# Graph layers on one core: the 0/1 matrices of destination lanes made in the attention loops, f32 sums without a split

## What is computed

```python
x = layernorm(x + segment_sum(exp(-weight)[:, None] * x[dst], src))         # messages, by source
q, k, v = x @ Wq.T + bq, x @ Wk.T + bk, x @ Wv.T + bv                        # 4 heads of 16
s = (sum(q[dst] * k[src]) / 4 + edge_attr @ We.T + be) * exp(log_temp)       # one score an edge and head
x = layernorm(x + layernorm(x + softmax_by_dst(s) * v[src] summed by dst, times Wo))
e = leaky_relu((x @ W_l)[src] + (x @ W_r)[dst], 0.2) @ att                   # second attention, one head
x = layernorm(x + softmax_by_dst(e) * (x @ W_l)[src] summed by dst + bias)
x = layernorm(x + two layers of mean over the neighbours)
```

## Time and profile before

| | |
|---|---|
| time, median of 3 runs | 5168.92 us (5147.55 to 5176.96) |
| profiled execution, first to last instruction | 3717.5 us |
| what the median has beyond that span | 1451.4 us |
| busy: TensorE, weight loads, VectorE, ScalarE, GpSimd | 58%, 44%, 70%, 21%, 53% |
| granted clock of TensorE, mean | 0.69 |
| message stage | about 205 to 715 us |
| sums by source | 715 to 1020 us |
| first attention stage | 1098 to 2204 us |
| second attention stage | 2327 to 3473 us |

### The profile page before, as it was taken

The page is one execution under the profiler, slowest core; times in us unless marked ns, Lnnn a source line. Parts: engine busy times, 40 slices in busy tenths (PEclk is TensorE's granted clock), DMA queues, the critical chain, the costliest instruction groups (busy, mean ns, idle before and its releaser), DMA issues. The chain is left out here.

```text
span 3717.5 us, 94213 instructions
## 1 busy us (share of the span) xinstructions
PE 2149.9 (58%) x24555; PEld 1628.6 (44%) x24556; DVE 2606.7 (70%) x5968; ACT 796.1 (21%) x2086; POOL 1984.6 (53%) x1987
## 2 busy tenths in 40 slices
PE   1435777566535555555655553465666666666597
PEld 0225666455534444444544442344444444444232
DVE  3898999888856777776777765477777777777511
ACT  0023555455520111111111110011111111111100
POOL 0112444333327777777777730777777777776000
PEclk9867889756655666666666665566666766666699
DMA  4046777788776667666666630565555555555687
GB/s 148 12 126 170 258 260 261 233 244 237 217 74 184 184 180 190 183 175 183 186 184 182 183 94 9 130 161 146 150 151 144 153 154 148 153 148 147 223 309 282
DMA packets 679457, 646.11 MB, mean 174 GB/s; under 512 B 129015, under 2 KB 513308, under 8 KB 678333
## 3 DMA queue, kind: packets, MB, share of 16 engines
q1 hardware_dynamic: 375773, 346.64, 31.7%
q0 software_dynamic: 77184, 154.07, 17.5%
q10 hardware_dynamic: 226300, 143.41, 12.6%
HBM read 433.64 MB, written 222.40 MB: 176 GB/s over the span
## 5 line engine op out<-in xcount | busy, mean ns | idle before, releaser
L1646 POOL DMA_INDIRECT rows<-nodes_xl,id_slot x832 | 831.1, 999 | 419.3 <-issue 249.5
L1646 POOL DMA_INDIRECT rows<-nodes_kv,id_slot x832 | 825.1, 992 | 290.8 <-issue 244.8
L1842 DVE SCALAR_TENSOR_TENSOR running_counts<-running_counts,same_block,counts_p 128x128 f32<-128x128 f32 x1144 | 393.9, 344 | 412.6 <-PE counts_p L2001 305.7
L2001 PE MATMUL counts_p<-hot_src,hot_blocks 128*128 128x128 bf16 x2288 | 291.9, 281 | 585.8 <-DVE running_counts L1842 584.4
L2001 PEld LDWEIGHTS counts_p<-hot_src,hot_blocks 128*128 128x128 bf16 x2288 | 217.6, 154 | 661.4 <-DVE running_counts L1842 599.4
L2045 PE MATMUL sums<-parts,hot 128*128 128x68 bf16 (+1 forms) x4992 | 325.2, 251 | 250.1 <-DVE parts L1826 250.1
L2045 PEld LDWEIGHTS sums<-parts,hot 128*128 128x128 bf16 x4992 | 311.6, 168 | 271.5 <-issue 271.5
L1091 POOL DMA_INDIRECT msg_by_src<-message,unit_slot x156 | 199.7, 1280 | 311.3 <-DVE message L944 292.4
L1260 PE MATMUL sums<-parts,hot 128*128 128x65 bf16 x3168 | 183.7, 235 | 120.7 <-DVE parts L1237 120.7
L1687 ACT CAST parts<-mixed 128x544 bf16<-128x544 f32 (+1 forms) x208 | 133.0, 639 | 536.1 <-DVE mixed L1810 278.1
L1971 PE MATMUL picked<-rows,ident 128*128 128x512 f32 x208 | 198.2, 1054 | 79.2 <-DMA rows<-nodes_xl,id_slot 68.3
(11 more groups left out here) (490 smaller groups left out, 4289.9 us busy)
## 6 DMA issues: line engine op xcount, KB each, us to landing
hot_src<-hot_src_by_cell SPq DMA_DIRECT2D x1144, 64.0 KB
adjacency<-running_counts ACTq DMA_DIRECT2D x1144, 64.0 KB
hotT<-hotT_by_step SPq DMA_DIRECT2D x208, 256.0 KB
hot<-hot_by_step SPq DMA_DIRECT2D x208, 256.0 KB
blocks<-adjacency SPq DMA_DIRECT2D x40, 1280.0 KB
hot_src_by_cell<-hot POOLq DMA_DIRECT2D x132, 256.0 KB
loc_all<-loc_by_cell SPq DMA_DIRECT2D x104, 256.0 KB
hotT_by_step<-hotT ACTq DMA_DIRECT2D x104, 256.0 KB
```

What stands on the lines that cost most here:

```text
L1646: pool.indirect_dma_start(out=rows[:, j, t, :], out_offset=None, in_=table, in_offset=bass.IndirectOffsetOnAxis(ap=ids[:, j, t:t + 1], axis=0)
L1842: v.scalar_tensor_tensor(runs[:, r, q, :], before_it, same[:, bass.ds(J * BBODY + (count_from + q), 1)], counts_p[:, q - HALVES[q >= len(H ...
L2001: ins = nc.tensor.matmul(counts_p[:, q - HALVES[half][0], :], hot_b[:, r, :, t], hot_s[:, r, q, :, g], start=g == 0, stop=g == 1)
```

## The change

In the message stage `build` and its stores go, with the loads of the lane rows and the constant `lane_h`. In the attention stages:

- `hotT`: SyncE loads the step's row of lanes, broadcast to all partitions (`loc_b`, 256 KB, in the place of the load of `hotT`; it waits only for the first of the two passes of four steps ago). ScalarE makes `hotT` in two passes over 1024 columns: |lane - partition|, then relu(1 - that). It does so two steps ahead, before the issue of the stores.
- `hot`: VectorE compares lanes with each edge's lane, written as f32 (128 x 1024), three steps after the step, right behind `hot_blocks`. The load of `hot` goes.
- `mixed` stays f32 and is the moving side of one f32 product a column: 8 f32 products in the place of 24 bf16 ones. `split`, `lowest_part` and ScalarE's copies go; `mixed` has four buffers, not two.
- `next_ids` runs four steps ahead, not two. ScalarE's loop leaves its last round of 8 steps outside.

```diff
@@ messages
-                    def loads(i):
-                        for q in range(NS):
-                            ...
-                            sp.dma_start(loc_all[:, q, :], loc_flat[:, bass.ds((i * NS + q) * (TB * P), TB * P)]
-                                         .to_broadcast([P, TB * P])).then_inc(loc_in[q], 16)
...
-                    def build(i, q):
-                        ...
-                        v.tensor_scalar(hotT[:, q, :], loc_all[:, q, :], part[:], None, ALU.is_equal).then_inc(hotT_made, 1)
-                        v.tensor_tensor(hot[:, q, :, :], lane_h[:], loc_h[...].to_broadcast([P, P, TB]), ALU.is_equal).then_inc(hot_made, 1)
...
-                    def store(i, q):
-                        ...
@@ attend, SyncE
-                                sp.wait_ge(products, J - 3)
-                            sp.dma_start(hotT[:, j % 4, :, :] ..., hotT_dram[bass.ds(J, 1), :, :] ...).then_inc(hotT_in[j % 4], 16)
-                            if w is not None:
-                                hot_load(w, 1 - j // 4, j % 4)
+                                sp.wait_ge(away_made, J - 3)
+                            sp.dma_start(loc_b[:, j % 4, :], loc_flat[:, bass.ds(J * (TB * P), TB * P)].to_broadcast([P, TB * P])
+                                         ).then_inc(loc_in[j % 4], 16)
@@ attend, ScalarE
+                        def lanes_hot(i, j):
+                            J = i * 8 + j
+                            act.wait_ge(minus_made, 1)
+                            act.wait_ge(loc_in[j % 4], (i * 2 + j // 4 + 1) * 16)
+                            if not (isinstance(i, int) and J == 0):
+                                act.wait_ge(hotT_made, J)
+                            nc.scalar.activation(away[:], loc_b[:, j % 4, :], ACT.Abs, bias=minus_part[:]).then_inc(away_made, 1)
+                            act.wait_ge(away_made, J + 1)
+                            if not (isinstance(i, int) and J < 4):
+                                act.wait_ge(products, J - 3)
+                            nc.scalar.activation(hotT[:, j % 4, :, :].rearrange("p t e -> p (t e)"), away[:], ACT.Relu, bias=1.0,
+                                                 scale=-1.0).then_inc(hotT_made, 1)
...
-                                next_ids(i, j + 2)
-                            if w is not None and s >= 2:
-                                ... (the copies of parts, L1687 and L1690)
+                                next_ids(i, j + 4)
+                                ahead = (i, j + 2) if j < 6 else (i + 1, j - 6)
+                                if live(ahead[0]):
+                                    lanes_hot(*ahead)
@@ attend, VectorE
-                        def split(w, q):
-                            ...
-                        def lowest_part(w, q):
-                            ...
+                        def edges_hot(i, j):
+                            J = i * 8 + j
+                            if not (isinstance(i, int) and J < 4):
+                                dve.wait_ge(scattered, J - 3)
+                            v.tensor_tensor(hot[:, j % 4, :, :], lane[:].unsqueeze(1).to_broadcast([P, TB, P]),
+                                            loc_h[:, bass.ds(J, 1), :].rearrange("p a t -> p (a t)").unsqueeze(2).to_broadcast([P, TB, P]),
+                                            ALU.is_equal).then_inc(hot_made, 1)
...
+                            if known_step(i, j - 3):
+                                edges_hot(i, j - 3)
@@ attend, TensorE
-                            pe.wait_ge(hot_in[p * 4 + q], use * 16)
-                            pe.wait_ge(low_made, J + 1)
+                            pe.wait_ge(hot_made, J + 1)
+                            pe.wait_ge(weighed, J * KM + KM)
                             for b, n in enumerate(ns):
                                 for t in (2 * b, 2 * b + 1):
-                                    for m in range(3):
-                                        ins = nc.tensor.matmul(sums[:, bass.ds(n, cols)], hot[:, p * 4 + q, :, t], parts[:, q % 2, m, t, :],
-                                                               start=False, stop=False)
+                                    ins = nc.tensor.matmul(sums[:, bass.ds(n, cols)], hot[:, q, t, :], mixed[:, q, t, :],
+                                                           start=False, stop=False)
```

More of the change, by code:

```diff
@@ L965, in step @@
                                 part_of(*at)
-                        if s in BUILD and inside(i):
-                            build(i, BUILD[s])
                     run(dve, step, lambda i: (later["tables"], later["links"], later["stairs"])[i](dve))
@@ L1076, in step @@
                                 part_of(*at)
-                        if s - 1 in BUILD and inside(i):
-                            store(i, BUILD[s - 1])
                     run(act, step)
-                    for q in range(NS):
-                        act.wait_ge(hot_kept[q], ROUNDS * 16)
-                        act.wait_ge(hotT_kept[q], ROUNDS * 16)
                 @block.gpsimd
@@ L1513, in attend @@
                 fade = sbuf("fade", [P, H], ctx=c)
[L1514 to L1517 removed]
+                mixed = sbuf("mixed", [P, 4, TB, cols], ctx=c)
+                hot = sbuf("hot", [P, 4, TB, P], ctx=c)
                 lane_b = sbuf("lane_b", [P, P, BT], BF16, ctx=c)
@@ L1551, in attend, with run @@
                 n_halves = len(HALVES)
-                def run(eng, step):
+                def run(eng, step, peel=0):
                     for j in range(8):
                         step(0, j)
-                    with eng.Fori(1, LOOPS) as i:
+                    with eng.Fori(1, LOOPS - peel) as i:
+                        for j in range(8):
+                            step(i, j)
+                    for i in range(LOOPS - peel, LOOPS):
                         for j in range(8):
```

124 lines of the change are left out of this document (31 added, 93 removed).

## The result

| | before | after |
|---|---|---|
| time, median | 5166.26 us (4 runs, 5147.55 to 5176.96) | 5271.65 us (4 runs, 5265.45 to 5278.19) |
| ratio | 1 | 1.0207, 95% interval 1.0177 to 1.0237 |

What follows compares the result with a forecast made beforehand. VectorE was taken to bound the message stage, gathers the first attention stage, their consumers the second. Terms -93 - 6 - 26 = -125 us gave a span of 3592 and a time of 5044 us, range 4990 to 5140.

Steps and rivals of the forecast that it cites:

- the median of the runs is 1451.4 us above it, and I take that as unchanged: Whole kernel: time beyond the profiled span of 3717.5 us lies outside it and stays the same.
- Rival (4): Whole kernel: the part outside the span scales with it, -174 us instead of -125, 4995 us; chance 0.08.
- three signs of being wrong: Gathers wait for `mixed` in both attention stages; scatter stays at clock 0.50; message stage stays above 460 us.
- The longer lead of the ids is worth nothing, since no wait of the gathers in the loop is for ids: Attention stages: making the ids four steps ahead instead of two changes the time by nothing.
- ScalarE: Attention stages: two passes of 1.1 us each replace two copies; cost 0, at most +1.2 us a window.
- Message stage, -93: Message stage: 104 builds leaving VectorE save 103 us, 10 given back to TensorE; ends -45 and -103.
- rival (1): Message stage: TensorE takes over as bound at 2.39 us a step; 5092 us, chance 0.13.
- Products, full clock: Attention stages: the f32 products run at full clock; two scatters cost 4.1 us there, 7.6 at half clock.
- Rival (2): Attention stages: f32 products run at 1.2 GHz throughout, 5280 us; chance 0.10, half of it for a mild form.
- Split and parts, -0.6 and -0.7 us a window: Attention windows: -0.6 us in the third step at full clock, -0.7 in the fourth as VectorE loses `left` and `parts`.
- Gathers' stretching: Attention stages: VectorE instructions lengthening gathers; `edges_hot` at 1.22 us replaces 1.40 us, so 0, ends +-15 us.

Runs made afterwards that it cites:

- e1: The kernel before, no edit, profiled again: 5194.72 us, span 5193.0 us.
- e16: e3 with the ids four steps ahead instead of two: 5235.68 us, 1.0136 of the kernel before.
- e3: The f32 sums part of the change alone, hotT still built in the message stage and loaded, ids two steps ahead: 4846.85 us, 0.9365 of the kernel before.
- e12: Changed kernel with hotT made by one VectorE comparison a step, row of lanes issued two steps sooner, no ScalarE passes: 5205.98 us, 1.0060 of the kernel before.
- e15: e12 with the ids two steps ahead instead of four: 4854.47 us, 0.9410 of the kernel before.
- e11: Changed kernel with the row of lanes issued two steps sooner and the passes last in ScalarE's step: 5177.10 us, 1.0000 of the kernel before.
- e17: e11 with the ids two steps ahead instead of four: 4848.27 us, 0.9409 of the kernel before.
- e2: Changed kernel with the ids two steps ahead instead of four: 5310.83 us (1 run), 1.027 of the kernel before.
- e6: Changed kernel once more, no edit: 5284.35 us, 1.0219 of the kernel before.
- e9: e3 plus two ScalarE passes of 1024 columns a step on a tile nobody waits for: 4863.72 us, 0.9398 of the kernel before.

## Why the prediction was wrong

**The step that failed first: "the median of the runs is 1451.4 us above it, and I take that as unchanged".** The time isn't outside but inside the attention stages (e1), in stretches in which instructions of the other engines come through only now and then while GpSimd issues gathers, and in the waits that follow from them. Rival (4), that this part follows the span, was the only place where it had a chance, and it expected the part to shrink. All that the prediction derives for the attention stages from the earlier trace rows (the gathers as the bound at 41.5 us a window, consumers at 42.2) belongs to an execution that the timed runs don't resemble: in them a window takes 69 us (1803 / 26). Two of its three signs of being wrong came: the gathers wait for `mixed` in both stages (807.4 and 774.2 us), and `scatter` ran at 0.50.

**The steps that made it slower: two terms put at nothing.** One is "The longer lead of the ids is worth nothing, since no wait of the gathers in the loop is for ids". In the trace that it was read from these waits are 9 us in 30 times. In the second trace they are 779 us in 57 times inside the stages, and they are useful: the ids are copied in ScalarE's queue, behind its other work, and so GpSimd stopped itself (that the gathers hold up this queue too is argued from the stretches above). Four steps ahead it stops only at the full ring. Shown with nothing else changed: +389 us (e16 to e3), 352 and 329 (e12 to e15, e11 to e17). The other is *ScalarE*, "0, with +1.2 us a window as the far end": with the ids two steps ahead, the row issued early and the passes last take 463 us off (e2 to e17), 8.9 us a window. The two prices don't add; either fault alone uses up the gain of the f32 sums (median us; e2 is a single run):

| | ids two ahead | ids four ahead |
|---|---|---|
| f32 sums, `hotT` still loaded | 4847 (e3) | 5236 (e16) |
| f32 sums, `hotT` in the loop, row early and passes last | 4848 (e17) | 5177 (e11) |
| f32 sums, `hotT` in the loop, row late and passes first | 5311 (e2) | 5284 (e6) |

**Message stage, -93: right in kind, its size within a third.** The first gather starts 84.8 us sooner than in the earlier trace rows (1098.7 less 1013.9), inside the ends of -45 and -103, but 120.6 sooner than in e1, past them: the window of the stage is 543 us there and not 510. A step of the changed kernel (TensorE, then VectorE):

```profile
452.13 0.45 PE L946 MATMUL sorted<-moved_fields,unit_hot 128*128 128x44 bf16 x6 [0.60 <-DVE unit_slot L904]
...
454.52 0.44 PE L946 MATMUL sorted<-moved_fields,unit_hot 128*128 128x44 bf16 x6
```

```profile
455.32 0.69 DVE L920 TENSOR_TENSOR message<-picked,w_slot 128x512 f32<-128x512 f32 x1 [0.68 <-PE picked L974]
```

TensorE needs its 2.39 us and VectorE then waits 0.68 us for it, as rival (1) had it for single steps; the clock rose as I had argued, to 0.89 (0.82 in the earlier trace rows, 0.73 in e1), and the stage took 427 us where some 415 were foreseen.

**Products, full clock: wrong.** Two `scatter`s take 7.09 us at a granted clock of 0.50, near the upper end of 4.1 to 7.6; over the whole run a pair keeps TensorE busy for 6.5 us on average (677.9 us in 104 pairs). Rival (2) said so and put 5280 us on it, within 10 us of the result. That the number is so near is luck, for it isn't the reason: e3 has the same products at the same clock and is 6% faster, and half of them left out gives 143 us, not 368.

**Split and parts, -0.6 and -0.7 us a window: far too small.** Their removal, with the loads of `hot`, is worth 265 us over 52 windows in e3, 5.1 us each. Which of the removed waits, copies and loads, or the two further buffers of `mixed`, carries it wasn't taken apart; argued, not shown: where an instruction comes through only every 0.7 us or a multiple of it, a chain VectorE - ScalarE - VectorE - ScalarE - VectorE - TensorE costs at each link.

**ScalarE: the length of the passes right, their place wrong.** They took 1.148 and 1.057 us (forecast 1.1 each). The estimate of 2.2 us for both from the figures of the Trainium skill (ScalarE: Activation LUTs, "What ACT_TABLE_LOAD costs") is met too. The Trainium skill's advice to put relu and additions on VectorE ("Rules for kernel authors" there) is about the time of one instruction, and so far the trace agrees: VectorE's one comparison in e12 takes 0.481 us. For the kernel's time it brings nothing here: VectorE in their place is no faster (e15 beside e17), and idle passes cost nothing that shows (e9). The row landed 3.1 us after its issue, not 2, and the exponentials came some 2.5 us late, as worked out; it costs 107 us (e11), 2.1 us a window, with the ids four steps ahead, past the far end of 1.2, and 463 us with two, as said above.

**Gathers' stretching: right.** Against the second trace of the kernel before they take 3.6 us more in the first stage (804.67 for 801.10) and 10.1 in the second (815.87 for 805.82), together near the upper end of +15. The rule of the Trainium skill, that a VectorE instruction with two SBUF inputs locks out a GpSimd operation that reads SBUF (SBUF — State Buffer, "SBUF: two separate sides"), fits single gathers: one at 2073.82 took 1.87 us beside the `hot` comparison of 2073.65 to 2074.87, and the longest took 2.0 us, where the kernel before had 1.65. On average it amounts to 8 ns a gather. The comparison itself took 1.22 us, as worked out.

In one line, by medians: before 5174; f32 sums 4847 (-327); ids four ahead 5236 (+389); `hotT` made in the loop on a late row, its build gone, 5284 (+49). The order decides whom the loss is put down to: with `hotT` first it is 5311 (+464, one run of e2), and then the ids give 5284 (-26, which one run can't tell from nothing).

## What to carry to other kernels

Look first whether the profiled span is near the measured time; where it isn't, profile again before working anything out, for here the difference was in the stages and not around them. An engine with long pauses may still cost its full length, if the others stand still while it works: look for short instructions that wait for nobody and come at even distances, and for the engine that is active just then. A wait that looks idle can be worth keeping: a longer lead, which took such waits away, cost 329 to 389 us here. Where two parts of a change can each hold up the same thing, try each with and without the other, for a single order of removing them gives the whole loss to one.

## What the runs showed of the hardware

- While GpSimd issued indirect gathers back to back (0.944 us each, 0.30 us between), from some 8 us on, products of 0.21 us came 2.1 us apart, four DMA issues of SyncE that take 1.85 us took 11.25, and a VectorE addition began 13.9 us after the products it waits for. For TensorE the trace shows no wait. Why stays open, and so does why one execution of the kernel before, at 3717.5 us, was free of it (1.4 us of such idle time before `picked`, 397.5 in its second trace) with 832 gathers in an unbroken series.
- Leaving out 768 of 1664 gathers with their transfers (each 1.25 us with its issue) saved 1015 us of a kernel whose GpSimd waited 1693 us.
- An f32 product of 66 or 68 columns with new weights took 0.44 us (7.09 us for 16) in a stage in which TensorE's clock was granted at 0.50.
